# Linear attention block: the numerators' state part as 32x32 tiles, and an order of work around it

## The reference

```
h = layernorm(x) * (1 + ca) + sa
q, k, v = split(h @ W_qkv + b_qkv)
q = elu(q / sqrt(32)) + 1.0001 ;  k = elu(k) + 1.0001
for each row t:   KV += k_t v_t^T (32x32 per head) ;  K += k_t
                  num = q_t KV ;  den = q_t . K + 1e-6 ;  a_t = num / den
x = x + ga * (a @ W_out + b_out)
x = x + gb * ffn(layernorm(x) * (1 + cb) + sb)      # gated ffn, hidden 1536, weights int / 127
```

## Time and profile before

| | us |
|---|---|
| median of 3 runs (lowest, highest) | 2092.07 (2091.65, 2092.77) |
| the profiled execution | 2091.66 |
| its span, first to last instruction | 2089.9 |
| PE busy in the span | 2056.5 (98%) |
| DVE busy | 1584.1 (76%) |
| ACT busy | 1004.8 (48%) |
| POOL busy | 978.5 (47%) |

### The profile page before, as it was taken

How to read it: one execution, slowest core, us unless ns; L and a number is a source line. 1 busy time by engine, 2 the same in 40 slices (tenths; PEclk the granted TensorE clock), 3 DMA queues, 4 the chain that set the end, 5 groups by cost and what they waited for, 6 DMA issues and landing times. The chain is left out here.

```text
span 2089.9 us, 41259 instructions
## 1 busy us (share of the span) xinstructions
PE 2056.5 (98%) x14852; PEld 1670.4 (80%) x14852; DVE 1584.1 (76%) x2160; ACT 1004.8 (48%) x1733; POOL 978.5 (47%) x782
## 2 busy tenths in 40 slices
PE   7999999999999999999998999999999999999999
PEld 4788888888888888888877888888888888888887
DVE  7998988989889889888885675757658575674744
ACT  5544554455544545444443643536445353643533
POOL 2644545555455454544543344443444434344444
PEclk9999999999999999999999999999999999999999
DMA  6012122221232212222155565564656546465543
GB/s 256 31 57 70 55 80 93 91 92 56 77 102 82 92 61 82 92 82 77 37 208 208 173 204 179 180 200 144 220 180 201 181 167 191 164 221 166 175 156 114
DMA packets 157151, 276.61 MB, mean 132 GB/s; under 512 B 11105, under 2 KB 35681, under 8 KB 157026
## 3 DMA queue, kind: packets, MB, share of 16 engines
q1 hardware_dynamic: 156498, 273.73, 40.0%
q10 hardware_dynamic: 528, 1.05, 0.1%
HBM read 208.67 MB, written 66.06 MB: 131 GB/s over the span
## 5 line engine op out<-in xcount | busy, mean ns | idle before, releaser
L1477 POOL TENSOR_TENSOR h_lo<-y_rows,h_hi 128x512 fp32r<-128x512 f32 x192 | 246.4, 1301 | 377.4 <-ACT h_hi L1575 377.3
L426 POOL TENSOR_TENSOR x_res<-y,x_res 128x512 f32<-128x512 f32 x64 | 83.1, 1298 | 305.4 <-DVE y L856 294.4
L833 DVE RECIPROCAL r_den<-r_den 128x512 f32<-128x512 f32 x64 | 213.8, 3342 | 1.0 <-ACT r_den L602 1.0
L589 ACT ACTIVATE z_exp<-pj,qk_neg 128x512 f32<-128x512 f32 x128 | 88.1, 688 | 210.1 <-PE pj L1104 175.8
L838 DVE TENSOR_TENSOR probs<-sc,causal 128x512 f32<-128x512 f32 x256 | 158.2, 678 | 0.8 <-PE sc L1132 0.8
L1104 PE MATMUL pj<-xt_hi,w_hi 128*128 128x512 f32 x512 | 149.8, 414 | 5.1 <-DVE v L828 2.1
L1901 PE MATMUL sc<-wd,h_hi 128*128 128x512 f32 x384 | 150.7, 392 | 0.0
L1901 PE MATMUL sc<-wd,h_lo 128*128 128x512 f32 x384 | 149.5, 389 | 0.0
L1104 PE MATMUL pj<-xt_lo,w_hi 128*128 128x512 f32 x512 | 138.8, 393 | 1.8 <-DVE xt_lo L805 1.8
L1690 DVE TENSOR_TENSOR r_den<-pj,k_tok 128x512 f32<-128x512 f32 x96 | 66.3, 690 | 97.2 <-ACT k_tok L1558 53.2
L1104 PE MATMUL pj<-xt_hi,w_lo 128*128 128x512 f32 x512 | 138.3, 392 | 0.0
(11 more groups left out here) (251 smaller groups left out, 5647.3 us busy)
## 6 DMA issues: line engine op xcount, KB each, us to landing
w_hi<-parts SPq DMA_DIRECT2D x48, 1024.0 KB, 5.3
w_lo<-parts SPq DMA_DIRECT2D x48, 1024.0 KB, 5.2
x_mid<-x_res SPq DMA_DIRECT2D x96, 256.0 KB, 2.1
x_res<-in_L_attn_x SPq DMA_DIRECT2D x64, 256.0 KB, 3.0
xg<-in_L_attn_x SPq DMA_DIRECT2D x15, 1024.0 KB, 6.6
x_res<-x_mid SPq DMA_DIRECT2D x60, 256.0 KB, 4.0
full<-x_mid SPq DMA_DIRECT2D x60, 256.0 KB, 3.8
parts<-r_den SPq DMA_DIRECT2D x48, 256.0 KB, 2.3
```

The costliest lines, as they stand in the source:

```text
L426: pool.tensor_tensor(out=x_res[:, slot, :], in0=y[:, :], in1=x_res[:, slot, :], op=ALU.add).then_inc(y_ready, 1)
L589: act.activation(z_exp[:, n % 2, :], pj[:, n % 2, :], ACT.Relu, bias=qk_neg[:, 1 - kind, c:c + 1], scale=-scale).then_inc(below_ready, 1)
L833: dve.reciprocal(r_den[parity][:, c, :], r_den[parity][:, c, :]).then_inc(rden_ready, 1)
L1477: pool.tensor_tensor(out=h_lo[b], in0=h[i], in1=h_hi[b].bitcast(F32), op=ALU.subtract).then_inc(h_lo_ready, 1)
```

## The change

The state part becomes 16 matmuls of 32x32 weights, one per chunk and head. Those of even chunks go to bank `num` at the head's own 32 partitions. Those of odd chunks go one place of 32 partitions further, into another bank (`odd_bank`: `sc[3]` for t = 0 and 1, `sc[2]` for t = 2 and 3, `pj[0]` in the last group), and so do the odd chunks' matmuls of the second part. The divide becomes two VectorE operations of 256 columns, one for each bank. The turned places are made good by a second block of ones for the denominators of odd chunks (`head_ones` has two blocks, set up at the start) and by the rows of W_out, which the host lays out in that order. New waits keep the borrowed bank apart from its other uses: scores wait for the divide of the tile before, numerators for one or all masks and for a denominator's copy.

Around it the order changes. TensorE: add_state comes directly behind numerators; denominators of t = 1 (counted for t = 2) and t = 2 (for t = 3) come ahead of out_project; the last denominators of a group move into the last projection unit, ahead of its last four passes, with a wait for the divide. ScalarE: `den_out` 1 ahead of `exp_relu` 7; `k_rows` ahead of `xt_high` for t = 2 and 3; the last `den_out` behind x and the state. The last two groups have their own variants. The order of DMAs is unchanged.

```diff
...
@@ -278,6 +277,24 @@
         return pj[:, 1, :] if isinstance(tile, int) and (NG - 1) * GT <= tile + 1 < NG * GT else y_bank
+
+    def odd_scores(tile, t):
+
+        if isinstance(tile, int) and tile >= (NG - 1) * GT - 1:
+            return 3 if tile < NG * GT - 1 else 0
+        return (3, 3, 2, 2)[t]
+
+    def odd_bank(tile, t):
+
+        if isinstance(tile, int) and (NG - 1) * GT <= tile < NG * GT - 1:
+            return turn_bank_of(tile)
+        return sc[:, odd_scores(tile, t), :]
+
+    def num_part(tile, t, c, h):
+
+        to = (h + c % 2) % HPC
+        bank = odd_bank(tile, t) if c % 2 else num
+        return bank[to * E:(to + 1) * E, c * P:(c + 1) * P]
 
@@ -716,15 +733,16 @@
                 exp_relu(n, 6)
-                exp_relu(n, 7)
                 if not isinstance(g, int):
...
                 den_out(n, other, 1, den_bank)
+                exp_relu(n, 7)
                 prod_high(n, 2)
...
                 xt_full(g + 2, 0, x_bank)
+            k_rows(g * GT + 2)
+            if two_ahead:
                 xt_high(g + 2, parity, 0)
-            k_rows(g * GT + 2)
             if last:
@@ -743,9 +761,10 @@
                 xt_full(g + 2, 2, x_bank)
-                xt_high(g + 2, parity, 2)
             if not last:
                 k_rows(g * GT + 3)
+            if two_ahead:
+                xt_high(g + 2, parity, 2)
             if last:
@@ -756,13 +775,16 @@
                 act.wait_ge(made_out[1], g * 16 + (-16))
-            if ahead:
+            near_last = isinstance(g, int) and g == NG - 2
+            if near_last:
                 den_out(n, other, 3, den_bank)
...
                 state_out(g * GT + 3)
+            if ahead and not near_last:
+                den_out(n, other, 3, den_bank)
 
@@ -844,9 +866,12 @@
             wait(dve, a_lo_ready, tile)
-            dve.tensor_tensor(out=a_t[:, :].rearrange("p (c i) -> p c i", c=C),
-                              in0=num[:, :].rearrange("p (c i) -> p c i", c=C),
-                              in1=r_den[parity][:, :, t * P:(t + 1) * P], op=ALU.mult).then_inc(a_ready, 1)
+            for odd, bank in enumerate((num, odd_bank(tile, t))):
+                ins = dve.tensor_tensor(out=a_t[:, :].rearrange("p (k e i) -> p e k i", e=2, k=2)[:, odd, :, :],
+                                        in0=bank[:, :].rearrange("p (k e i) -> p e k i", e=2, k=2)[:, odd, :, :],
+                                        in1=r_den[parity][:, :, t * P:(t + 1) * P]
+                                        .rearrange("p (k e) i -> p e k i", e=2)[:, odd, :, :], op=ALU.mult)
+            ins.then_inc(a_ready, 1)
 
@@ -887,11 +912,14 @@
         dve.memset(half_neg[:, :], -0.5)
-        link(dve.memset(head_diag[:, :], 0.0))
-        for h in range(HPC):
-            ins = dve.memset(head_diag[h * E:(h + 1) * E, h * E:(h + 1) * E], 1.0)
+        same_head = junk[:, 0:2 * P].rearrange("p (e n) -> p e n", e=2)
+        link(dve.memset(same_head, 0.0))
+        for odd in range(2):
+            for h in range(HPC):
+                to = (h + odd) % HPC
+                ins = dve.memset(same_head[h * E:(h + 1) * E, odd, to * E:(to + 1) * E], 1.0)
         link(ins)
-        dve.tensor_copy(head_ones[:, :], head_diag[:, :])
+        link(dve.tensor_copy(head_ones[:, :, :], same_head))
         dve.memset(ones[:, :], 1.0)
...
@@ -1087,6 +1115,12 @@
             for i, (hi_w, hi_x, k) in enumerate(passes):
+                if i == 2 * C and u == UNITS - 1 and not (isinstance(g, int) and g == 0):
+                    wait(pe, a_ready, g * GT)
+                    if isinstance(g, int) and g == NG - 1:
+                        x_turn(NG, 3, x_bank)
+                    else:
+                        denominators(g, 3, den_bank)
                 w = w_hi if hi_w else w_lo
@@ -1108,14 +1142,15 @@
             wait(pe, den_ready, g * C + c)
-            pe.matmul(bank, head_ones[:, :], prod_hi[:, :], start=True, stop=False)
-            pe.matmul(bank, head_ones[:, :], prod_lo[:, :], start=False, stop=True).then_inc(den_ps, 1)
+            pe.matmul(bank, head_ones[:, c % 2, :], prod_hi[:, :], start=True, stop=False)
+            pe.matmul(bank, head_ones[:, c % 2, :], prod_lo[:, :], start=False, stop=True).then_inc(den_ps, 1)
 
...
             wait(pe, y_gated, min(tile - 1, (NG - 1) * GT - 1) if isinstance(tile, int) else tile - 1)
+            wait(pe, a_ready, min(tile, (NG - 1) * GT) if isinstance(tile, int) else tile)
             wait(pe, ktok_ready, tile)
@@ -1146,16 +1181,26 @@
         def numerators(tile, g, parity, t):
             wait(pe, kv_ready, tile)
             wait(pe, a_ready, tile)
+            if isinstance(tile, int) and (NG - 1) * GT <= tile < NG * GT - 1:
+                pe.wait_ge(ktok_ready, tile + 1)
+            else:
+                wait(pe, probs_ready, tile * HPC + odd_scores(tile, t) + 1)
+            if isinstance(tile, int) and tile == (NG - 1) * GT - 1:
+                pe.wait_ge(xf_ready, NG * C + 3)
+            elif t >= 2 and (not isinstance(g, int) or g + 1 < NG):
+                wait(pe, den_ready, (g + 1) * C + t)
             for c in range(C):
-                pe.matmul(num[:, c * P:(c + 1) * P], kv_diag[:, c, :], qt[parity][:, c, t * P:(t + 1) * P],
-                          start=(c == 0), stop=False, skip_group_check=True)
+                for h in range(HPC):
+                    rows = slice(h * E, (h + 1) * E)
+                    pe.matmul(num_part(tile, t, c, h), kv_diag[rows, c, rows], qt[parity][rows, c, t * P:(t + 1) * P],
+                              start=(c < 2), stop=False, skip_group_check=True)
             wait(pe, v_ready, g * C + t + 1)
             wait(pe, probs_ready, (tile + 1) * HPC)
             for c in range(C):
                 for h in range(HPC):
                     f = c * P + h * E
-                    mm = pe.matmul(num[h * E:(h + 1) * E, c * P:(c + 1) * P], v[parity][:, t, f:f + E],
-                                   probs[:, h, c * P:(c + 1) * P], start=False, stop=(c == C - 1),
+                    mm = pe.matmul(num_part(tile, t, c, h), v[parity][:, t, f:f + E],
+                                   probs[:, h, c * P:(c + 1) * P], start=False, stop=(c >= 2),
                                    skip_group_check=True)
             mm.then_inc(num_ready, 1)
 
@@ -1231,17 +1276,21 @@
         def rest(g, parity, t):
             tile = g * GT + t
             ahead = not isinstance(g, int) or g + 1 < NG
-            if t == 3 and ahead:
+            near_last = isinstance(g, int) and g == NG - 2 and t == 3
+            if t >= 2 and ahead:
                 wait(pe, probs_ready, tile * HPC + 3)
-                denominators(g + 1, 2, den_bank)
+                denominators(g + 1, t - 1, den_bank)
+            if near_last:
+                pe.wait_ge(probs_ready, tile * HPC + 4)
+                x_turn(g + 2, 2, x_bank)
             if not ahead and t + 1 < GT:
                 k_turn(tile, parity, t)
             if not isinstance(tile, int) or tile > 0:
                 out_project(tile - 1)
-            if t in (1, 2) and ahead:
+            if t == 1 and ahead:
                 wait(pe, probs_ready, tile * HPC + 3)
-                denominators(g + 1, t - 1, den_bank)
-            if t >= 2 and (not isinstance(g, int) or g + 2 <= NG):
+                denominators(g + 1, 0, den_bank)
+            if t >= 2 and (not isinstance(g, int) or g + 2 <= NG) and not near_last:
                 wait(pe, probs_ready, tile * HPC + 4)
                 x_turn(g + 2, 2 * t - 4, x_bank)
             if ahead:
...
@@ -1257,13 +1306,15 @@
             numerators(tile, g, parity, t)
-            if t == 3 and ahead:
+            if ahead:
+                add_state(tile, parity, t)
+            if near_last:
                 denominators(g + 1, 3, den_bank)
-            if t >= 2 and (not isinstance(g, int) or g + 2 <= NG):
+            elif t >= 2 and (not isinstance(g, int) or g + 2 <= NG):
                 x_turn(g + 2, 2 * t - 3, x_bank)
...
                 project(g + 1, 1 - parity, 3 * t + 2)
-            if ahead or t + 1 < GT:
+            if not ahead and t + 1 < GT:
                 add_state(tile, parity, t)
@@ -1291,7 +1342,7 @@
                 if t == GT - 1:
-                    pe.wait_ge(ktok_ready, NG * GT - 1)
+                    pe.wait_ge(a_ready, NG * GT - 1)
                     first_product()
@@ -2014,6 +2065,9 @@
             a = a.reshape(C, P)
+        if name == "L0_attn_W_out":
+            a = a.reshape(C // 2, 2, HPC, E, D)
+            a = np.stack([a[:, 0], np.roll(a[:, 1], 1, axis=1)], axis=1).reshape(D, D)
         layouts = [(f"in_{name}", a.T if name in _TURNED else a)]
```

More of the change, by code:

```diff
@@ L124, in build @@
         causal = sbuf(top, "causal", [P, P])
-        head_diag = sbuf(top, "head_diag", [P, P])
-        head_ones = sbuf(top, "head_ones", [P, P], F32R)
+        head_ones = sbuf(top, "head_ones", [P, 2, P], F32R)
         c_col = sbuf(top, "c_col", [P, C])
```

(8 more changed lines are left out.)

## The result

The changed kernel takes 2077.23 us (median of 4 runs, 2074.96 to 2079.39) by 2092.42 for the kernel before on the same chip (4 runs, 2091.65 to 2094.13): ratio 0.9929, interval 0.9917 to 0.9941. It is faster by 15.2 us, inside the predicted range, where I forecast 24. The profiled execution of it, the slowest of its four, took 2079.39 us, 12.3 less than that of before, with a span of 2077.7; sums over its parts answer to this 12.3.

A forecast was written before the change was run, and what follows sets the result against it. TensorE was taken to bound the attention. Tile savings -28.5, mask waits +5.2, group ends -3.5, first group +2.7 and +0.3 summed to -23.8 us, giving 2068 us; range 2062 to 2085.

The forecast's parts named there:

- The state part: TensorE's 32x32 matmuls run eight at once, four rounds of 0.11 us; 0.559 against 0.893: -0.334 us a tile.
- add_state: Directly behind the numerators it saves one switch of tile shape and a first load: -0.119 us in 60 tiles.
- wait on k_tok: add_state needs k_tok earlier; no wait taken, but without the reordering's cover up to 0.4 us in a quarter of tiles.
- the last denominators' copy: At a group's end ScalarE copies them later, to about 592.3, scores want them near 592.5: no wait taken, cover 0.2 us.
- The mask wait of t = 2: TensorE's denominators wait for VectorE's third mask, 0.26 us plus an open load of 0.11: +0.37 us in 14 groups.
- The end of a group: TensorE's loss waiting for v falls from 0.44 to 0.17 us as den_out leaves the chain: -0.27 us a group.
- The group's sum: A group falls from near 64.8 us to 63.1: -1.81 from TensorE's savings, +0.37 and -0.27 from waits.
- The first group: Tile 1's scores wait for tile 0's divide: +3.5 us, swallowing an old wait, so +2.7, and +0.3 for a mask wait.
- Five rounds: Rival 1: a matmul's two records follow each other on one tile, state part 0.55 not 0.44 us: 2075 us, chance 0.14.
- taking turns: Rival 4: tiles writing one bank take turns, two records at a time in the state part: 2149 us, chance 0.07.
- rival 3: State part runs four tiles at a time at most, +6.8 us, offset by other savings: 2091 us, chance 0.08.
- rival 2: VectorE or ScalarE ends last more often, each of 16 groups giving back 0.8 us: 2081 us, chance 0.15.

The follow-up runs named there:

- add_state put back alone: Changed kernel with add_state again behind the third projection unit and ScalarE's last denominators ahead of the state's copy: 2080.74 us, 0.9945 of before.
- changed kernel again: The changed kernel, unaltered, run once more beside the variants: 2077.53 us, 0.9932 of the kernel before.
- bias earlier: Changed kernel with GpSimd adding the bias to the group's last residual ahead of a_low of t = 3, not behind it: 2067.41 us.
- before, bias earlier: Kernel before, with only GpSimd's bias addition for the group's last tile moved ahead of a_low of t = 3: 2085.88 us, 0.9967 of before.
- reciprocals earlier: Changed kernel with the first group's two late reciprocals moved ahead of the first feature: 2073.85 us, 0.9912 of the kernel before.
- one bank: Changed kernel with all chunks' 32x32 matmuls unrotated on tiles (h, h) and in bank num: 2097.88 us, 1.0030 of the kernel before.
- new order alone: Changed kernel with the state part back to 128x128 matmuls in one bank, unrotated; new order, waits and two-operation divide stay: 2091.34 us, 0.9999 of before.
- norm_x later: Changed kernel with VectorE's layernorm of x moved behind the masks of t = 2: 2074.57 us, 0.9917 of the kernel before.
- all three: Changed kernel with bias earlier, first reciprocals earlier and layernorm of x behind the masks together: 2060.95 us; the same with the 128x128 state part: 2077.76 us.

## Why the prediction was right, and where it was wrong

**The state part: right in mechanism, a little short in size.** Eight tiles at a time, four rounds of 0.11. It saves 0.277 us a tile, by 0.334. The four rounds' 0.44 was right. The changes of tile shape cost more than I took: behind the part 0.60 - 0.44 = 0.16 us, where I had 0.092; in front of it 0.09 (0.53 us from k_turn's start to the part's, by 0.44 before), where I had 0.119 with a load. That leaves 0.99 - 0.60 - 0.09 = 0.30, of which 0.277 arrives; where the rest goes I can't say.

**add_state: right in kind, short in size.** One stretch of narrow matmuls fewer saves 0.093 by 0.119 a tile (this takes all of the new order in; add_state put back alone costs 0.067 in t = 1 and 0.10 in t = 3). The two shortfalls are (0.334 - 0.277) + (0.119 - 0.093) = 0.083 a tile, 0.33 a group. No wait on k_tok came but once, 0.3 us, nor one on the last denominators' copy in any group.

**The mask wait of t = 2: right.** +0.30 us in group 8, 0.25 in the mean of groups 1 to 14, by +0.37. By my own sum it follows from the smaller savings: TensorE arrives 0.37 earlier and not 0.453, so 0.18 of delay and 0.11 of open load.

**The end of a group: the step that failed.** I wrote: "The chain is divide, a_hi, den_out, xf, xt_hi, xt_lo, reciprocal, v. den_out leaves it", -0.27 us. den_out does leave ScalarE's part, and xt_lo does become ready earlier (in the changed kernel 1.2 us before scores, 0.9 before), but its end is set by GpSimd: divide, a_hi, a_lo, add_bias, and VectorE's xt_lo not before 0.55 us after that. The change took nothing out of that chain and put the 0.07 of the second divide into it, while TensorE came earlier. The loss at v is what taking GpSimd's addition away gives: 0.45 us before and 0.70 after, so +0.25, not -0.27. 0.52 in 13 groups are 6.8 us; the profiled execution lies 11.5 us above the forecast, the median 9. The sign to see was in the timeline of before: an xt_lo of 1.33 us at 591.77, and one of 0.68 at 589.18, of the same shape. I used its end and never asked why it was twice as long.

**The group's sum.** Measured term by term: -4 x 0.277 - 4 x 0.093 + 0.30 + 0.25 = -0.93; measured directly -0.97; forecast -1.71. In 14 groups the difference is 10 us, most of what the forecast missed.

**The first group: the wait right, its after-effect missed.** Tile 0 takes 19.23 us by 16.19 before: +3.04, where 3.5 - 0.453 = 3.05 had been forecast. Both profiles have 3.4 us at the lower clock in this tile. In profiles without them it takes 18.0 to 18.1 (changed kernel again, bias earlier) by 14.54 (before, bias earlier), so +3.5: the agreement holds for profiles of one kind. The prediction read the page's forty 9s as a clock granted in full, but a 9 stands for 90% or more. In these 10 us of the kernel before the mean granted clock is 0.83 (last columns: clock, DMA share, GB/s):

```profile
74.00:84.00 10.00, 7.98 (x44) 6.27 (x38) 6.44 (x11) 2.06 (x5) 7.42 (x6) 0.83 0.15 55
```

The lower clock that followed the wait was not forecast: tile 1 takes 16.91 in the changed kernel and 15.27 with the reciprocals earlier, +1.6.

**The rivals.** Five rounds and taking turns fell with the bursts of eight. Four at a time is what the tiles on the diagonal in one bank give, but rival 3 put that kernel at 2091 and it takes 2098. The state part's price was right in it (+6.5 us between the two kernels of one bank, by +6.8), the 7.9 us that the rest was to save were not (0.3 with the new order alone). Of rival 2 a part came true: one of the engines behind did end last, in 13 groups, at 0.52 us and not 0.8, and by a meeting of two engines rather than by VectorE's load. The range was drawn wide for rivals 1 and 2, and the time lies in it at a point that neither of them describes; that it lies inside is in part luck.

## What to carry to other kernels

An instruction that takes twice the time of the shortest of its kind in the same timeline may be waiting without a wait being shown: look which other engine runs beside it before building a chain through it, and move that one into an idle stretch. Here a GpSimd addition moved some 3 us earlier was worth two thirds of what the change brought. Price a saving against the engine behind it, since it ends at the first wait that stays, and price a new wait like the one of some 3 us here with the clock that may fall after it. Small matmuls on the diagonal of the array gain nothing by themselves (1.01 us by 0.99): here it took a second set of tiles, rotated by one and writing a second bank.

## What the hardware showed that I had not expected

- VectorE's subtraction with both inputs in SBUF (xt_lo) took 1.85, 1.33 and 0.69 us, by how much of a GpSimd operation of 1.3 us still lay ahead when it started. It was not the only one. Of the four xt_lo of a group three end 0.55 us after a GpSimd operation, before and after the change, and take 1.3 to 1.9 us; only the fourth, with no GpSimd operation beside it, takes 0.68. The addition for v, one input of it in PSUM, is not touched: the one at 642.82 takes 0.68 us though a GpSimd operation runs beside it from 642.31 to 644.05. The feature's kt, with both inputs in SBUF too, meets another of GpSimd's bias additions in the same way (changed kernel; it ends at 623.07, GpSimd at 622.52; the shortest kt takes 0.62):

```profile
621.03 1.49 POOL L437 TENSOR_TENSOR x_res<-x_res,gabo_row 128x512 f32<-128x512 f32 x1
621.27 1.80 DVE L835 SCALAR_TENSOR_TENSOR kt<-z_relu,z_exp 128x512 f32<-128x512 f32 x1
```

- In five of the seven profiles in which scores waited 2.8 to 3.8 us for the first divide (the changed kernel, again, add_state back, bias earlier, norm_x later) the granted clock fell to half at 92.4 to 94.4 us, for about 3.4 us; in the other two (one bank, new order alone) it did not. It fell there neither in the kernel before nor in the four without that wait (first reciprocals earlier, all three with either state part, before with the bias earlier). The waits were 2.93, 3.34, 3.75, 3.36 and 3.31 us in the five and 2.83 and 2.90 in the two; 2.90 and 2.93 lie too close to make a rule of it. A stretch at the lower clock from 77 to 78 us on stands in four profiles (before, the changed kernel, one bank, new order alone) and does not tell them apart either. What does was not tried.
- Eight 32x32 tiles of fp32 ran at a time, four to each of two banks, with 0.11 us a round, the same as four tiles of 128x32.

Not tried: den_out moved behind xf in the kernel before alone, which would price its part of ScalarE's chain once GpSimd is out of the way.
